# Summing the exponentials of an attention group: full-width products at every second key tile in place of half-width products at every tile

## The reference

```python
scores = jnp.einsum('bhsd,bhtd->bhst', q, k) / scale       # s: 512 queries, t: 1601 keys
scores = jnp.clip(scores, -50.0, 50.0)
scores = jnp.where(attend, scores, -10000.0)
scores = jnp.clip(scores, -50.0, 50.0)
probs = jax.nn.softmax(scores, axis=-1)
ctx = jnp.einsum('bhst,bhtd->bhsd', probs, v)
```

## Time and profile before

| | |
|---|---|
| time, median of 3 runs | 1475.78 us (1474.55 to 1476.06) |
| profiled execution, its own time | 1475.65 us |
| its span, first to last instruction | 1473.8 us |
| granted TensorE clock, mean | 0.989 |
| busy share of the span: PE, PEld, DVE, ACT, POOL | 97%, 65%, 75%, 55%, 6% |
| first attention stage, first scores to the next stage's first product | 146.59 to 274.85 us |
| the others | from 370.74, 592.30 and 813.91 us |

### The profile page before, as it was taken

How to read it: one execution, slowest core, us unless ns; L and a number is a source line. 1 busy time by engine, 2 the same in 40 slices (tenths; PEclk the granted TensorE clock), 3 DMA queues, 4 the chain that set the end, 5 groups by cost and what they waited for, 6 DMA issues and landing times. The chain is left out here.

```text
span 1473.8 us, 25109 instructions
## 1 busy us (share of the span) xinstructions
PE 1424.8 (97%) x10352; PEld 955.6 (65%) x10352; DVE 1108.7 (75%) x1657; ACT 815.1 (55%) x1018; POOL 88.9 (6%) x128
## 2 busy tenths in 40 slices
PE   5999999999999999999999999998999999999997
PEld 5887333688333688333588333576788888888886
DVE  5953899895899885799885799887765565656554
ACT  4343899535899635899634899534432333333330
POOL 1000000101000100000100000110010010000100
PEclk9999999999999999999999999999999999999999
DMA  8453000436100425100424500362345544455435
GB/s 270 149 189 143 9 10 10 148 104 203 79 17 10 138 84 192 36 17 10 137 79 179 226 16 10 95 236 84 143 150 203 189 173 146 157 205 178 171 143 171
DMA packets 54785, 180.91 MB, mean 123 GB/s; under 512 B 11168, under 2 KB 25760, under 8 KB 42384
## 3 DMA queue, kind: packets, MB, share of 16 engines
q1 hardware_dynamic: 39696, 116.08, 21.9%
q0 software_dynamic: 14976, 63.23, 12.7%
HBM read 111.97 MB, written 67.31 MB: 122 GB/s over the span
## 5 line engine op out<-in xcount | busy, mean ns | idle before, releaser
L944 ACT ACTIVATE cx_probs<-cx_sc,proj_mbias 128x1024 f32<-128x1024 f32 (+1 forms) x416 | 442.7, 1114 | 45.7 <-PE cx_sc L1211 38.1
L1089 DVE TENSOR_SCALAR cx_probs<-cx_probs 128x1024 f32<-128x1024 f32 (+1 forms) x416 | 269.9, 684 | 57.1 <-ACT cx_probs L944 55.7
L1051 DVE TENSOR_TENSOR cx_padd<-cx_probs,cx_probs 128x1024 f32<-128x1024 f32 x192 | 233.6, 1217 | 1.1 <-DVE cx_probs L1089 0.2
L1211 PEld LDWEIGHTS cx_sc<-cx_q,cx_kt 32*128 32x128 f32 (+1 forms) x2496 | 103.6, 183 | 198.3 <-ACT cx_probs L944 181.3
L1224 PE MATMUL cx_acc<-cx_probs,cx_vt 128*32 128x512 f32 (+1 forms) x1664 | 220.9, 603 | 3.7 <-DVE cx_probs L1089 3.7
L1211 PE MATMUL cx_sc<-cx_q,cx_kt 32*128 32x512 f32 (+1 forms) x2496 | 206.5, 433 | 14.5 <-ACT cx_probs L944 11.1
L136 PE MATMUL cx_sc<-proj_cs,proj_wk 128*128 128x256 f32 (+1 forms) x1152 | 149.1, 289 | 11.1 <-DVE proj_wk L599 11.1
L136 PEld LDWEIGHTS cx_sc<-proj_cs,proj_wk 128*128 128x128 f32 x1152 | 145.4, 190 | 15.3 <-issue 14.2
L136 PE MATMUL cx_sc<-proj_wv,proj_cs 128*128 128x512 f32 (+1 forms) x624 | 149.6, 396 | 1.2 <-DVE cx_kt L1036 1.2
L136 PE MATMUL ff_yp<-hand_wds,ff_held 128*128 128x512 f32 x624 | 147.9, 395 | 0.1
L1686 DVE TENSOR_TENSOR ff_x<-ff_yp,ff_x 128x512 f32<-128x512 f32 x128 | 85.6, 689 | 75.0 <-PE ff_yp L136 62.1
(11 more groups left out here) (286 smaller groups left out, 1776.9 us busy)
## 6 DMA issues: line engine op xcount, KB each, us to landing
ff_x<-scr_x SPq DMA_DIRECT2D x32, 1024.0 KB, 5.0
scr_x<-ff_x SPq DMA_DIRECT2D x28, 1024.0 KB, 4.9
proj_raw<-in_ctxT SPq DMA_DIRECT2D x20, 512.0 KB, 4.9
hand_wds<-scr_wd POOLq DMA_DIRECT2D x7, 1024.0 KB, 10.1
scr_q<-cx_q SPq DMA_DIRECT2D x3, 2048.0 KB, 7.2
cx_wo<-scr_wo POOLq DMA_DIRECT2D x3, 2048.0 KB, 13.7
scr_xs<-cx_xs POOLq DMA_DIRECT2D x3, 2048.0 KB, 7.9
cx_q<-scr_q SPq DMA_DIRECT2D x3, 1536.0 KB, 10.9
```

The costliest lines, as they stand in the source:

```text
L944: nc.scalar.activation(prob(N)[0:r], sc[n % NSC][0:r], ACT.Exp, bias=mbias[0:r, b, t:t + 1], scale=SCALE).then_inc(exp_done, 1)
L1051: nc.vector.tensor_tensor(padd[z][(g * QP + j) % 2][:], prob(2 * i + z)[:], prob(2 * i + 2 + z)[:], ALU.add).then_inc(added[z], 1)
L1089: nc.vector.tensor_scalar(prob(N)[0:r], prob(N)[0:r], LOW, HIGH, ALU.max, ALU.min).then_inc(clip_done, 1)
L1211: last = nc.tensor.matmul(sc[(2 * i + h // 2) % NSC][0:r, h % 2], kt[own, z, c, t * P:t * P + r], q[own, y, c], start=n == 0, stop=n == 2)
```

## The change

`sums` loses its argument `half` and takes all 512 columns in one call: 4 matmuls with 512 columns in place of twice 4 with 256. `weigh` calls it ahead of the values of the tiles 4, 6, 8, 10 and 12 (j = 0 to 4), and at tile 2 of the next group for j = 5; in the last group of a stage the call for j = 5 follows all steps. At tile 12 a full call, the values and `single` come in one step. `owed` is gone. The counts of `sums_done` go with it. The additions on VectorE and their buffers are as before.

```diff
-    SUMS = 2 * QP + 1
+    SUMS = QP + 1
...
         def sums_until(g, j):
 
-            return g * SUMS + 2 * j + 2 + (1 if j >= QP - 2 else 0)
-
-        SINGLE = 2 * QP - 2
+            return g * SUMS + j + 1 + (1 if j == QP - 1 else 0)
+
+        SINGLE = QP
...
-                def sums(b, c, j, half):
+                def sums(b, c, j):
                     g = b * HC + c
-                    if j == 0 and half == 0:
+                    if j == 0:
                         at_least(pe, tot_out, g)
                     for z in range(2):
                         pe.wait_ge(added[z], g * QP + j + 1)
-                    cols = slice(half * S // 2, (half + 1) * S // 2)
                     for h in range(HC):
-                        last = nc.tensor.matmul(tot[h * HD:(h + 1) * HD, cols], ones[:], padd[h // 2][(g * QP + j) % 2][:, h % 2, cols],
-                                                start=j == 0 and half == 0, stop=j == QP - 1 and half == 1)
+                        last = nc.tensor.matmul(tot[h * HD:(h + 1) * HD], ones[:], padd[h // 2][(g * QP + j) % 2][:, h % 2],
+                                                start=j == 0, stop=j == QP - 1)
                     last.then_inc(sums_done, 1)
...
                 def weigh(b, i):
                     c, t = divmod(i, TT)
-                    if t < 3 and c:
-                        owed(b, c - 1, t)
-                    if 3 <= t < TT - 1:
-                        sums(b, c, (t - 3) // 2, (t - 3) % 2)
+                    if t == 2 and c:
+                        sums(b, c - 1, QP - 1)
+                    if t >= 4 and t % 2 == 0:
+                        sums(b, c, t // 2 - 2)
                     values(b, i)
                     if t == TT - 1:
                         single(b, c)
-
-                def owed(b, c, n):
-                    sums(b, c, QP - 2 + (n + 1) // 2, (n + 1) % 2)
...
                     weigh(b, STEPS - 1)
-                    for n in range(3):
-                        owed(b, HC - 1, n)
+                    sums(b, HC - 1, QP - 1)
```

## The result

The changed kernel takes 1496.84 us (median of 4 runs, 1491.99 to 1500.05), the kernel before 1475.92 beside it. The ratio is 1.0140, with a 95% interval from 1.0123 to 1.0158: slower by 21 us. A second set gave 1496.79 and a ratio of 1.0152 (1.0130 to 1.0173). The profiled execution shown here took 1495.43 us.

A forecast was written before the change was run, and what follows sets the result against it. TensorE's work was taken to bound nearly every step, just above a 2.17 us loop with ScalarE's exponentials through PSUM. Four stages at 5.84 us add 23.4 to 1475.65, giving 1499.0 us, range 1490 to 1509.

The forecast's parts named there:

- The two limits: Each step takes the larger of TensorE's own work and 2.17 us, the loop from scores through exponential to next scores.
- Long and short steps: Steps with a full call take 2.76 us, those without sums 2.17, a pair 4.93 instead of 4.66.
- Rival A: Only TensorE's work counts: long and short steps even out, a pair takes 4.63 us, total 1470.8; chance 0.05.
- rival D: Calls are not bunched as read, or a wait holds them elsewhere: within 0.2% of before; chance 0.02.
- One sign: A whole group should take 32.6 us with about 2.1 us of TensorE idle in it.
- The full call costs 0.89, saving 0.03 a pair: One full call of sums costs TensorE 0.89 us against 0.92 for two half calls.
- The subtraction 2.33 - 0.46: Step with a half call less that call: a step without sums has 1.87 us of TensorE work.
- The end of a stage: From last scores to next stage, 7.69 us becomes 7.17 as the full call nearly fills a 0.92 wait: gain 0.5.
- Waits that move: Later copies on ScalarE cost nothing; VectorE's additions wait for later sums within 0.25 us of slack per pair.
- Rival B: VectorE becomes the bound as additions wait for later sums: a pair takes 5.08 us, +14, total 1513; chance 0.07.
- The sum: Per stage 1.08 + 2 x 1.92 + 1.42 - 0.5 = 5.84 us; four stages 23.4 us.
- Rival C: TensorE's clock lapses once in each of 12 later groups, 1.87 of work taking 3.42: +15 us, 1514; chance 0.03.

The follow-up runs named there:

- the threshold between 192 and 128 columns: Kernel before with a pair's two half calls made uneven: 192 and 320 columns, ratio 1.0006; 128 and 384 columns, ratio 1.0030.
- the exponentials of three widths: Kernel before and changed kernel with exponentials over 256 or 384 of 512 queries from a stage's fifth tile; with 256, 1467.13 and 1471.38 us.
- the run with 384 queries: Kernel before and changed kernel with exponentials over 384 of each head's 512 queries from a stage's fifth tile: 1470.37 and 1478.43 us.

## Why the prediction was right, point by point

**The two limits.** TensorE's work and the loop of 2.17 us: shown, by the threshold between 192 and 128 columns and by the exponentials of three widths. That the loop, and not ScalarE's rate, is the second limit rests on the run with 384 queries; the rows behind the prediction could not tell, and it didn't ask.

**Long and short steps.** Forecast 2.76, 2.17 and 3.65, measured 2.75 to 2.76, 2.17 to 2.18 and 3.62. A group was forecast at 32.58 and takes 32.56; the first group's part 19.66 and takes 19.65; the last's 29.88 and takes 29.89. From the sixth step to the last scores that is 6.34 a stage, or 25.4 over four, and 25.4 was measured. Rival A, by which short steps take 1.87, and rival D, by which the calls are not bunched, are excluded by these rows.

One sign was put too high: a group should have had some 2.1 us of TensorE idle and has 1.45. The short step of 2.17 has 1.90 of work, not 1.87, and of the 0.27 that is left the last values' drain covers a part, so that 0.21 is marked as idle.

**The full call costs 0.89, saving 0.03 a pair.** The price was right, the saving was not. It is the one term of the steps' sums that was mis-sized. With short exponentials a step without sums has 1.90 us of work and not 1.87, so that a pair is 2.76 + 1.90 = 4.66, just what two steps of 2.33 were. Whichever call comes first behind the scores costs 0.03 more: values behind sums take 0.97 to the next scores (192.85 to 193.82), values straight behind scores 1.00 (194.72 to 195.72). It also makes the step at the change of group 3.62 and not 3.65: the values there cost 0.86 behind the full call (180.93 to 181.79), where they had cost 0.89 behind the scores (180.60 to 181.49). The subtraction 2.33 - 0.46 missed that. The error didn't touch the forecast, since short steps were at 2.17 either way, but it overpriced rival A, which would have had only the stages' ends to gain.

**The end of a stage.** Forecast 0.5 less each, measured 0.45 to 0.47. The new end was put at 7.17 and is 7.24: the last full call takes 0.97 to the next stage's products (278.26 to 279.23), not 0.89.

**Waits that move.** ScalarE's copy of `acc` was to start 0.89 later against its scores:

```profile
182.04 0.60 ACT L922 ACTIVATE cx_ob<-cx_acc 128x512 f32<-128x512 f32 x1 [0.77 <-PE cx_acc L1224]
```

It starts 2.90 after the scores of 179.14, where it was 2.04, so 0.86 later, and waits 0.77; the scores behind it were not late. VectorE's additions were to wait up to 0.25 a pair for the sums:

```profile
189.22 1.23 DVE L1051 TENSOR_TENSOR cx_padd<-cx_probs,cx_probs 128x1024 f32<-128x1024 f32 x1 [0.18 <-PE cx_tot L1235]
```

They do, 0.16 to 0.18 us a pair in this group, 9.6 in 54 waits in all. But in the changed kernel's list of waits no exponential waits for an addition (in that of before 8 did, for 3.1 us). Rival B, in which VectorE becomes the bound, has its wait and not its price: the wait lies in VectorE's slack.

**The sum.** 23.4 us forecast; the stages without their first steps give 23.5. The two profiled executions differ by 19.8, because the kernel before had lost 2.0 us more in the first steps of its stages and had started its first stage 1.5 later. The medians differ by 20.9, for which no trace gives the parts. Such differences between executions were in no term of the sum; the range held them with room to spare. Rival C, a lapse of the clock in the steady part, was not seen: in a whole group it is 1.00. Its price was about right: in the kernel before the step from 375.57 us, at a granted clock of 0.50, takes 3.45, where the rival had 3.42. The Trainium skill's 60 cycles for each matmul (TensorEngine Tiling (Array Packing), Instruction Overhead), by which 768 fewer records would save an estimated 19 us, do not show here as a cost of each record: 16 records of 256 columns and 8 of 512 both cost 0.88 to 0.89 us, at 4 products side by side.

## What to carry to other kernels

When an engine is full and a loop with another engine lies just under its step, count the work step by step: each step costs the larger of its work and the loop, so moving the same work into fewer, heavier steps loses what the light steps then wait, and gets nothing back in the heavy ones. Spread such work so that every step stays above the loop's time; down to there unevenness is free. A wait that is already there, as at the end of a stage, is the place for work that can be moved.

## What the runs showed of the hardware

Most of the spread between runs of the kernel before goes with the granted clock of TensorE: its mean was 0.993 in the fastest of 17 runs, 1471.56 us, and 0.988 in the slowest, 1481.53, and a straight line on it accounts for about three quarters of the spread in these runs. At a stage's start TensorE waits twice for 1.2 of 2.2 us, and in the next steps runs at half the clock, in some executions for one step and in others for two or three: the first five steps took between 10.87 and 13.15 us. That the waits bring the fall on is shown by the products put into them: in 12 stages traced with them there is none. Ten products of no use a stage, in waits that are there anyway, bring back about 8 us of 1476; they lengthen the two steps by 0.1 us each, since five of them take 1.36 us to the next scores and not the 1.1 that was expected. The same fall is left elsewhere; in the profiled execution with those products it came in a projection after the last stage, after TensorE had waited 4 us for VectorE:

```profile
965.00:970.00 5.00, 1.01 (x6) 0.51 (x4) 3.88 (x7) 0.00 (x0) 0.00 (x0) 0.83 1.00 371
970.00:975.00 5.00, 5.00 (x12) 3.94 (x13) 2.31 (x4) 0.00 (x0) 0.00 (x0) 0.50 1.01 423
```

A call of four products, each in its own 32 columns of the array, costs by the columns that they stream: 128, 192, 256, 320, 384 and 512 columns took 0.24, 0.35, 0.46, 0.56, 0.67 and 0.89 us to the start of the next call, behind scores.
